# Second cross attention: the rotary factors loaded first, and the first group's tiles summed, normed and turned into queries one at a time

## What is computed

```
x = x + cross_attention_0(ctx, norm(x), mask)        keyed, rms-normed
x = x + self_attention_0(norm(x))
x = x + mixture_of_experts(norm(x))                  top 8, capacity 128
x = x + cross_attention_1(norm(x), ctx)              <- the change is here
x = x + self_attention_1(norm(x))                    with rotary positions
x = x + tanh_map(norm(x))
```

```
q = einsum('bsf,fhd->bshd', norm(x), wq) / sqrt(64)
k = einsum('bsf,fhd->bshd', ctx, wk);  v = einsum('bsf,fhd->bshd', ctx, wv)
y = einsum('bhqk,bkhd->bqhd', softmax(einsum('bqhd,bkhd->bhqk', q, k)), v)
out = einsum('bqhd,hdo->bqo', y, wo) + bo
```

## Time and profile before

| | before |
|---|---|
| three runs | 2632.19, 2638.38, 2640.3 us; median 2638.38 |
| profiled execution | 2634.05 us, span of its instructions 2632.3 us |
| busy: TensorE, VectorE, ScalarE, GpSimd | 2440.3, 1697.8, 1281.7, 1476.0 us |
| granted clock of TensorE, mean | 0.965 |

### The profile page before, as it was taken

One profiled execution on the slowest core, in us unless ns is written; L12 is line 12 of the kernel. 1 busy time (PEld: TensorE's weight loads), 2 busy tenths in 40 slices (PEclk: granted clock), 3 DMA queues, 4 the chain that ended last, 5 costly groups with the idle time before them and its releaser, 6 DMA issues. The chain is left out here.

```text
span 2632.3 us, 64303 instructions
## 1 busy us (share of the span) xinstructions
PE 2440.3 (93%) x24481; PEld 1902.7 (72%) x24481; DVE 1697.8 (65%) x3969; ACT 1281.7 (49%) x2969; POOL 1476.0 (56%) x1674
## 2 busy tenths in 40 slices
PE   6898999999999999997887998599999999998997
PEld 3457788788787888785565588478888888885665
DVE  5676868686867777774575834466556655653665
ACT  3565656565656565563442323244454445543343
POOL 6896757576767576763771244565456545332333
PEclk9999999999999999998897999699999999999998
DMA  4232212111112111110003368532234323210001
GB/s 167 114 142 73 62 34 49 36 44 40 45 34 50 35 45 40 40 32 8 30 4 130 105 200 289 174 112 79 68 95 103 75 68 93 71 45 15 3 3 35
DMA packets 223075, 190.04 MB, mean 72 GB/s; under 512 B 88705, under 2 KB 210514, under 8 KB 222770
## 3 DMA queue, kind: packets, MB, share of 16 engines
q1 hardware_dynamic: 206386, 151.19, 19.2%
q0 software_dynamic: 10080, 30.00, 4.5%
q10 hardware_dynamic: 6304, 4.72, 0.6%
HBM read 151.53 MB, written 34.31 MB: 71 GB/s over the span
## 5 line engine op out<-in xcount | busy, mean ns | idle before, releaser
L288 POOL TENSOR_TENSOR rk<-ss,neg_half 128x32 f32<-128x32 f32 x64 | 348.6, 5447 | 247.6 <-DVE ss L270 247.6
L1745 PE MATMUL banks<-rowsT,qk 128*128 128x257 f32 x1024 | 243.4, 380 | 0.9 <-ACT qk L1672 0.9
L321 ACT ACTIVATE ksq<-kT 128x512 f32<-128x512 f32 x256 | 161.1, 629 | 160.4 <-DVE kT L264 160.4
L264 DVE COPY kT<-banks 128x512 f32<-128x512 f32 x256 | 177.0, 692 | 60.8 <-PE banks L375 56.7
L375 PE MATMUL banks<-x_hi,wk_hi 128*128 128x256 f32 x1024 | 213.5, 289 | 1.1 <-DVE kT L264 1.0
L1745 PEld LDWEIGHTS banks<-rowsT,qk 128*128 128x128 f32 x1024 | 189.6, 190 | 27.6 <-ACT qk L1672 1.2
L375 PE MATMUL banks<-x_hi,wk_lo 128*128 128x256 f32 x1024 | 206.7, 284 | 0.0
L375 PE MATMUL banks<-x_lo,wk_hi 128*128 128x256 f32 x1024 | 205.6, 282 | 0.3 <-DVE x_lo L256 0.3
L1222 ACT ACTIVATE score<-score,ntop 128x289 f32<-128x289 f32 x256 | 135.4, 530 | 115.6 <-DVE ntop L1103 115.4
L1593 POOL CAST r_hi<-diff 128x512 fp32r<-128x512 f32 x64 | 41.6, 650 | 258.0 <-PE banks L1771 257.2
L1566 POOL DMA_INDIRECT parts<-scratch_expert,address x128 | 132.2, 1033 | 93.2 <-DVE residual L1464 45.6
(11 more groups left out here) (369 smaller groups left out, 6538.1 us busy)
## 6 DMA issues: line engine op xcount, KB each, us to landing
rowsT<-in_ctxT SPq DMA_DIRECT2D x64, 257.0 KB, 2.9
wgu<-in_expert_gu SPq DMA_DIRECT2D x64, 256.0 KB, 3.9
rows<-in_ctx SPq DMA_DIRECT2D x64, 256.0 KB, 3.1
raw<-in_ctx SPq DMA_DIRECT2D x61, 256.0 KB, 2.7
scratch_qT<-qT SPq DMA_DIRECT2D x16, 512.0 KB, 2.6
scratch_kT<-kT SPq DMA_DIRECT2D x16, 512.0 KB, 3.0
q<-scratch_qT SPq DMA_DIRECT2D x64, 128.0 KB
kT<-scratch_kT SPq DMA_DIRECT2D x64, 128.0 KB
```

The costliest lines, as they stand in the source:

```text
L264: nc.vector.tensor_copy(m.kT[:, k, 2 * i:2 * i + 2, 0:ROWS], banks[i % 2].rearrange("p (a r) -> p a r", a=2)).then_inc(s.kT, 1)
L288: nc.gpsimd.tensor_tensor(m.rk[:], m.ss[:], kit.neg_half[:, 0:KF * H], ALU.pow).then_inc(s.rk, 1)
L321: nc.scalar.activation(m.ksq[:, 2 * i:2 * i + 2, :], m.kT[:, k, 2 * i:2 * i + 2, 0:ROWS], ACT.Square).then_inc(s.ksq, 1)
L1745: mm = nc.tensor.matmul(score[h][:, c - h * HALF, 0:CTX], m.qk[:, f, j, c * BT:(c + 1) * BT, :].rearrange("p h q -> p (h q)"), m.rowsT[:, ...
```

## The change

Four things change in the prologue of `cross_plain`:

- SP waits, behind wq, until the rotary factors are in (`rotary.count`, which is 16 x 11); then it loads wkT and bo, then rows 0 and rows 1.
- The two tiles of group 0 go one after the other through total, added, root (`inverse`), normed rows, transposes and query products. The functions get a counter u (how many times they have run) and `tiles` (which columns they take); `turn(g)` = g + 1 is the count for group g, since group 0 uses two. On GpSimd the first root stands between the fifth and the sixth gather of tile 1, the second ahead of `differences` of batch 0.
- wkT isn't scaled any more; the factor 1/8 is put into the copies of the queries out of PSUM, which become multiplications, in all groups.
- The rotary splits change places: `high` on ScalarE behind tile 0's query copies; `rest` (VectorE) and `mid` (ScalarE) behind tile 1's query copies and ahead of the copies of qk; `low` behind those.

The diff, without its renamings in the loop and in `RotaryProducts`:

```diff
+        ALL = range(GN)
+
+        def turn(g):
+
+            return g + 1
+
+        def span(tiles):
+
+            return slice(tiles.start * P, tiles.stop * P)
...
                 sp.dma_start(m.wq[:], w_q.rearrange("(f p) n -> p f n", p=P)).then_inc(s.w_in, 16)
+
+                sp.wait_ge(rotary.s.loaded, rotary.count)
+                weights.load_first(sp, d.bo1, d.wkT1)
                 rows(0)
-                weights.load_first(sp, d.bo1, d.wkT1)
                 rows(1)
...
-                def normed_rows(g):
-                    dve.wait_ge(s.rstd, g + 1)
-
-                    past(dve, s.xlT_ps, g)
-                    for i in range(GN):
+                def normed_rows(g, u, tiles):
+                    dve.wait_ge(s.rstd, u + 1)
+
+                    if g > 0:
+                        dve.wait_ge(s.xlT_ps, u)
+                    for i in tiles:
                         norm.rows(m.xl[:, i, :], g * GN + i, m.rstd[:, i:i + 1]).then_inc(s.xl, 1)

-                def queries_T(g, i):
-                    dve.wait_ge(s.q_ps, g * 4 + i)
-                    nc.vector.tensor_copy(m.qT[:, 2 * i - 2:2 * i, :].rearrange("p a t -> p (a t)"), kit.psum(7)).then_inc(s.q_dve, 1)
+                def queries_T(u, i, tiles):
+                    dve.wait_ge(s.q_ps, u * 4 + i)
+                    nc.vector.tensor_scalar(m.qT[:, 2 * i - 2:2 * i, span(tiles)], kit.psum(7).rearrange("p (a t) -> p a t", a=2)[:, :, span(tiles)],
+                                            DH ** -0.5, None, ALU.mult).then_inc(s.q_dve, 1)
...
-                dve.wait_ge(weights.first, weights.first_count)
-                nc.vector.tensor_scalar(wkT[:], wkT[:], DH ** -0.5, None, ALU.mult).then_inc(s.wkT, 1)
                 rotary.take(dve)
-                total(0)
-                added(0)
-                rotary.biases(dve)
+                for i in ALL:
+                    total(i)
+                    added(i)
+                    normed_rows(0, i, range(i, i + 1))
+                    if i == 0:
+                        rotary.biases(dve)
+                    queries_T(i, 2, range(i, i + 1))
+                    queries_T(i, 4, range(i, i + 1))
                 rotary.rest(dve)
-                total(1)
-                added(1)
-                normed_rows(0)
+                queries(0)
                 rotary.low(dve)
-                queries_T(0, 2)
-                queries_T(0, 4)
-                queries(0)
                 maxima(0, 0)
                 softmax(0)
...
-                def inverse(g):
-                    pool.wait_ge(norm.s.kept, (g + 1) * GN)
+                def inverse(g, u, tiles):
+                    first, end = g * GN + tiles.start, g * GN + tiles.stop
+                    pool.wait_ge(norm.s.kept, end)

                     past(pool, s.xl, g * GN)
-                    inv_root(nc, pool, kit.neg_half[:, 0:GN], m.rstd[:], norm.m.mv[:, g * GN:(g + 1) * GN, 1], 1.0, LN_EPS, ALU.add, s.eps, g + 1, s.rstd)
+                    inv_root(nc, pool, kit.neg_half[:, 0:end - first], m.rstd[:, tiles.start:tiles.stop], norm.m.mv[:, first:end, 1], 1.0, LN_EPS, ALU.add,
+                             s.eps, u + 1, s.rstd)
...
-                for t in range(GN):
-                    for c in range(TOPK):
-                        gather(t, c)
+                for c in range(TOPK):
+                    gather(0, c)
+
+                for c in range(TOPK):
+                    if c == 5:
+                        inverse(0, 0, range(0, 1))
+                    gather(1, c)
                 turning.zero(pool)
+                inverse(0, 1, range(1, 2))
                 for n in range(2):
                     differences(n)
                     parts(n)
-                inverse(0)
                 pool.wait_ge(weights.first, weights.first_count)
                 bias(0)
                 for c in range(TOPK):
...
-                def rows_T(g):
-                    act.wait_ge(s.xlT_ps, g + 1)
-                    nc.scalar.copy(m.xlT[:], kit.psum(6).rearrange("p (f t) -> p f t", f=FC)).then_inc(s.xlT, 1)
-
-                def queries_T(g, i):
-                    act.wait_ge(s.q_ps, g * 4 + i)
-                    nc.scalar.copy(m.qT[:, 2 * i - 2:2 * i, :].rearrange("p a t -> p (a t)"), kit.psum(6)).then_inc(s.q_act, 1)
+                def rows_T(u, tiles):
+                    act.wait_ge(s.xlT_ps, u + 1)
+                    nc.scalar.copy(m.xlT[:, :, span(tiles)], kit.psum(6).rearrange("p (f t) -> p f t", f=FC)[:, :, span(tiles)]).then_inc(s.xlT, 1)
+
+                def queries_T(u, i, tiles):
+                    act.wait_ge(s.q_ps, u * 4 + i)
+                    nc.scalar.mul(m.qT[:, 2 * i - 2:2 * i, span(tiles)], kit.psum(6).rearrange("p (a t) -> p a t", a=2)[:, :, span(tiles)], DH ** -0.5).then_inc(s.q_act, 1)
...
                 rotary.take_rest(act)
-                rotary.high(act)
+                for i in ALL:
+                    rows_T(i, range(i, i + 1))
+                    queries_T(i, 1, range(i, i + 1))
+                    queries_T(i, 3, range(i, i + 1))
+                    if i == 0:
+                        rotary.high(act)
                 rotary.mid(act)
-                rows_T(0)
-                queries_T(0, 1)
-                queries_T(0, 3)
                 queries(0)
...
-                def rows_T(g, n):
-                    pe.wait_ge(s.xl, (g + 1) * GN)
+                def rows_T(g, tiles, n):
+                    pe.wait_ge(s.xl, g * GN + tiles.stop)

                     past(pe, s.mix0, n)
+                    if g == 0:
+                        past(pe, s.q_act, 2 * tiles.start)
                     for f in range(FC):
-                        for i in range(GN):
+                        for i in tiles:
                             mm = nc.tensor.transpose(kit.psum(6)[:, f * GT + i * P:f * GT + (i + 1) * P], m.xl[:, i, f * P:(f + 1) * P], kit.ident[:])
                     mm.then_inc(s.xlT_ps, 1)

-                def queries_T(g, i, n):
-
-                    pe.wait_ge(s.xlT, g + 1)
+                def queries_T(u, i, tiles, n):
+
+                    pe.wait_ge(s.xlT, u + 1)

                     past(pe, (s.mix0, s.mix1)[(i - 1) % 2], n)
                     if i > 2:
-                        pe.wait_ge((s.q_act, s.q_dve)[(i - 1) % 2], g * 2 + 1)
+                        pe.wait_ge((s.q_act, s.q_dve)[(i - 1) % 2], u * 2 + 1)
+                    elif i == 2:
+                        past(pe, s.q_dve, u * 2)
                     for pr in (2 * i - 2, 2 * i - 1):
                         for f in range(FC):
-                            mm = nc.tensor.matmul(kit.psum(7 - i % 2)[:, pr % 2 * GT:(pr % 2 + 1) * GT], m.wq[:, f, pr * P:(pr + 1) * P], m.xlT[:, f, :],
-                                                  start=(f == 0), stop=(f == FC - 1))
+                            mm = nc.tensor.matmul(kit.psum(7 - i % 2)[:, pr % 2 * GT + tiles.start * P:pr % 2 * GT + tiles.stop * P], m.wq[:, f, pr * P:(pr + 1) * P],
+                                                  m.xlT[:, f, span(tiles)], start=(f == 0), stop=(f == FC - 1), skip_group_check=True)
                     mm.then_inc(s.q_ps, 1)
...
                 def queries(g):
                     for pr in range(NP_):
                         if pr % 2 == 0:
-                            pe.wait_ge((s.q_act, s.q_dve)[pr // 2 % 2], g * 2 + pr // 4 + 1)
+                            pe.wait_ge((s.q_act, s.q_dve)[pr // 2 % 2], turn(g) * 2 + pr // 4 + 1)
...
-                rows_T(0, 0)
-                for i in range(1, 5):
-                    queries_T(0, i, 0)
-                pe.wait_ge(s.wkT, 1)
+                for tile in ALL:
+                    rows_T(0, range(tile, tile + 1), 0)
+                    for i in range(1, 5):
+                        queries_T(tile, i, range(tile, tile + 1), 0)
+
+                pe.wait_ge(rotary.s.ready, 3)
+                pe.wait_ge(weights.first, weights.first_count)
                 queries(0)
                 scores(0, 0)
                 scores(0, 1)
```

37 lines of the change are left out of this document (19 added, 18 removed).

## The result

The changed kernel takes 2620.77 us (median of six runs, 2619.67 to 2625.11); the kernel before took 2635.78 us beside it (six runs, 2630.95 to 2640.3). The ratio is 0.9948, 95% interval 0.9938 to 0.9959: 15.0 us or 0.5% faster by the medians, 13.4 us by the two profiled executions (2634.05 and 2620.7 us; spans 2632.3 and 2618.9). Forecast were 6.7 us, 2631.7, with a range that ended at 2624: the sign was the one that follows from the steps, the size was not, and the time lies outside the range.

A forecast was written before the change was run, and what follows sets the result against it. TensorE idles in two holes, the first until the rotary loads land. Scores at 1653.5 + 33.9 + 10.3 + 1.2 = 1698.9 against 1705.6, 6.7 us less: 2631.7 from the median 2638.38; range 2624 to 2639.

The forecast's parts named there:

- Part 1, the order of loads: Rotary loads ahead of wkT, bo and rows on SP: they are in at 1653.5 instead of 1663.5, 10 us earlier.
- L: The moment at which the rotary loads are in: 1663.5 before, forecast 1653.5, bounds 1651.5 and 1657.
- two allowances: In the rotary load time: 1.9 us until data flow and 0.8 us for the last landing, both guesses.
- Rival A: Rotary load bound by its own small packets: L = 1657.5, 2.7 us less, 2635.7; chance 0.18.
- D: Rival: order of loads does nothing since gathers fill the engines; 3.3 us more, 2641.7; chance 0.04.
- Part 2, tile 0: Group 0's first tile: queries start at L + 14.1 and take 5.5 us, bounds 4 and 8.
- Part 3, tile 1: Group 0's second tile: queries start at 1680.3, take 7.1 us, end at L + 33.9 against L + 34.1 before.
- The split itself gains nothing by my count: Tiles one after the other: no gain, for a second slow start and a fold that waits for matmuls.
- Part 4: rotary.rest and mid ahead of the keys' copies: TensorE stalls 2.3 us, and lower clock behind costs 1.2, bounds 0 to 3.
- Part 5: Items priced at nothing: wkT's scaling, GpSimd's moved differences, second weights, query copies as multiplications, rotary.low under the first scores.

The follow-up runs named there:

- the runs without the split: Kernel before with new load order, factor 1/8 in query copies and GpSimd's root first: 0.9959; plus SP issuing the turning loads: 0.9966, with 34 useless products too 0.9928.
- the kernel before with 17 products: Kernel before plus 17 useless 32x32 matrix products on TensorE ahead of the rotary products, 68 instructions as the split added: 0.9978 of the kernel before.
- order only: Kernel before with the new load order and the factor 1/8 in the query copies, both tiles together as before: 0.9974 of the kernel before.

## Why the prediction was wrong

**Part 1, the order of loads: right.** L moved by 10.8 us in the absolute, 10.0 was forecast. The two allowances were guesses and their sum was 0.8 us too long. That the rotary queue takes 3.55 us of all engines stood (3.5). A reason was missed: before, ACT's issues took up to 3.16 us each, and without SP's loads beside them they ended 5 us sooner. Rival A (small packets) fell, D too.

**Part 2, tile 0: right** in the first profile, L + 13.8 and 5.2 us; the two others have L + 14.1 and 15.8, and 6.5 and 6.4 us, within its bounds of 4 and 8.

**Part 3, tile 1: the start right in the first profile, the size wrong.** 7.1 us were forecast with the low clock for 6.2 us from the queries' first matmul. The low stretch was 6.8 us long but began with the transposes' wait, 3.3 us ahead of the queries, so 3.5 us of it fell on them: 5.5 us. That is the largest of the three corrections up to the scores: with L 0.8 us sooner, 1.5 us less for the queries and 0.6 more for the clock, 6.7 becomes 8.4. The first profile is the luckiest of three here: in the second and third tile 1 starts at L + 28.6 and L + 30.1 and takes 6.2 and 6.1 us, and the scores start at L + 47.0 and L + 49.0, where 45.4 was forecast and the first has 44.5. So up to the scores the forecast lies inside the scatter. "The split itself gains nothing by my count" held in the runs without the split: their first scores come 2 to 5 us sooner in one chip's comparison and two us later in another's.

**Part 4: right** in its stall (2.3 us, 2.31 measured) and its cause; the clock behind it cost 1.8 us instead of 1.2 (12.2 us from the end of the queries to the scores, less the 8.0 of before and the stall), within the bounds.

**Part 5: right but for one item.** Rotary.low, the table load, the differences and the second weights ended no wait of TensorE up to the first scores. VectorE's `xl` of tile 1 took longer beside GpSimd's differences, which had moved there:

```profile
1665.08 0.41 DVE L156 TENSOR_SCALAR xl<-residual,mv,rstd 128x256 f32<-128x256 f32 x1 [0.99 <-POOL rstd L122]
...
1677.07 1.35 DVE L156 TENSOR_SCALAR xl<-residual,mv,rstd 128x256 f32<-128x256 f32 x1 [0.98 <-POOL rstd L122]
```

0.94 us on the path, priced at nothing. The start of tile 1's queries met the forecast all the same, since the fold ahead of it had begun 0.7 us sooner than forecast (L + 19.4, not L + 20.1): two misses that cancel. The Trainium skill (Trainium Architecture — The Big Picture, What this means for kernel authors) says that VectorE and GpSimd share one port pair under an exclusive lock. The trace agrees that the two hinder each other: GpSimd's `diff` started at 1677.02, 0.05 us ahead of the slow one. In the other 12 traces in which it does so, that `xl` takes 1.35 or 1.36 us as well; in the five in which `diff` runs elsewhere every `xl` there takes 0.40 to 0.42. Whether it is a lock no trace here tells.

**The step that failed** is a sentence of the first paragraph: "Behind the start of the scores, 1705.63 now, the order of work stays as it is, so the question is when the scores of batch 0 start." The order did stay, and its time was put at nothing all the same. The split's 68 instructions moved the blocks in which TensorE's program arrives. In the run that moves them and changes nothing else, the kernel before with 17 products, this is worth 0.9978, 5.8 us (2 to 9 by the interval), with 3.3 of them behind the last scores by its trace; in the changed kernel it is 3.1 us there in both pairs of profiles. The rest was not located in a trace. The other side of the sum is order only, 0.9974, which is 6.9 us: what the forecast said the whole change would give. Together they make 12.7 of the 13.7 us.

The time itself was 10.9 us under the forecast, and not all of that is this step. 2.6 us are the base: the forecast set out from 2638.38, the median of three runs, and the six beside the changed kernel give 2635.78. By the first pair of profiles 1.7 are the scores' start, 1.9 the part between first and last scores, 3.1 the part behind; 1.6 are the difference between medians and profiles.

**The range** took its bounds from the terms of the sum and the scatter of the runs, and nothing for the case that instructions elsewhere change their time. The time came out 3.2 us below 2624, which is less than the 17 products alone are worth.

## What to carry to other kernels

Before pricing an edit by its stage, count the instructions that it adds to or takes from each engine's stream, and look behind the stage for idle time on `issue` inside runs of equal short matmuls: an edit moves these boundaries, and 68 useless instructions were worth 5.8 us here, where the whole change was worth 13.7. When a gain is larger than its steps, split the change on the chip and pad the other half to the same instruction count before crediting the order of work. And look for DMA issues in the queue of an engine that computes: moving 13 of them to SP, one line, took 3.5 to 5.7 us out of the first step, more than was ever shown for the split's own order of work.

## What the runs showed of the hardware

- TensorE's program came in transfers of 16 KB, 256 instructions of 64 bytes, during the run; nine fetches in ten took 0.9 to 1.5 us, and where it started only as TensorE ran dry the pause was 2.7 us. All 45 pauses of over 1 us for `issue` between weight loads of one kind, behind 1700 us in 18 traces, ended 1.2 to 1.6 us after the end of a transfer. Why some fetches start ahead and others don't was not found.
- With the DMA engines 0.83 to 0.86 busy, TensorE executed one to three small products and then idled 0.3 to 1.2 us, again and again, in one kernel on one chip.
- An issue of a DMA on ACT took mostly 0.44 us in the row of 13, and up to 3.16 us with SP's loads queued.
- A 128x256 VectorE operation took 1.35 us where a GpSimd tensor operation had started 0.05 us ahead of it, and 0.40 to 0.48 otherwise.
